# A decoder kernel on one core: the linear layer in fives and the turnings, products and low parts at other steps of a 32-step turn

## The reference, cut to what matters

```python
out = jnp.einsum('bsk,nk->bsn', data, w) + bias              # linear layer, w with blocks masked
scores = jnp.einsum('bsgrd,btgd->bgrst', xq, xk) / math.sqrt(HEAD_DIM)
probs = jax.nn.softmax(scores + mask, axis=-1)
out = jnp.einsum('bgrst,btgd->bsgrd', probs, xv)             # cross attention, 32 heads
rq = (hidden_states @ Wq.T) @ Wr.T                           # slot memory: route, take the best 8 of 256 slots
learned = gelu(h @ Wu1.T + bu1) @ Wu2.T + bu2                # its uncertainty
```

## Time and profile before

| | us |
|---|---|
| median of 3 runs | 3841.97 (3831.95 to 3848.12) |
| the profiled execution | 3841.48 |
| its span, first to last instruction | 3839.7 |
| TensorE busy | 3357.9 (87%) |
| VectorE busy | 1858.2 (48%) |
| ScalarE busy | 1296.8 (34%) |
| GpSimd busy | 826.6 (22%) |

### The profile page before, as it was taken

How to read it: one execution, slowest core, us unless ns; L and a number is a source line. 1 busy time by engine, 2 the same in 40 slices (tenths; PEclk the granted TensorE clock), 3 DMA queues, 4 the chain that set the end, 5 groups by cost and what they waited for, 6 DMA issues and landing times. The chain is left out here.

```text
span 3839.7 us, 65645 instructions
## 1 busy us (share of the span) xinstructions
PE 3357.9 (87%) x25342; PEld 2694.0 (70%) x25342; DVE 1858.2 (48%) x4790; ACT 1296.8 (34%) x3539; POOL 826.6 (22%) x700
## 2 busy tenths in 40 slices
PE   2888999987489999999947999999998299999997
PEld 2677777776278887888825878888886177777775
DVE  4577777776522222333224233332223377777775
ACT  1566666665211011111101111110111276666663
POOL 1122122211043222233202323333222000000000
PEclk9899999998599999999966999999999599999998
DMA  5756566562121111111022111111111565455541
GB/s 181 179 144 151 155 151 163 153 156 67 46 77 52 42 39 46 40 55 55 33 55 66 44 49 55 55 55 44 38 44 26 150 146 128 128 128 127 128 123 40
DMA packets 189980, 346.44 MB, mean 90 GB/s; under 512 B 27873, under 2 KB 145217, under 8 KB 189778
## 3 DMA queue, kind: packets, MB, share of 16 engines
q1 hardware_dynamic: 186032, 341.00, 33.1%
q10 hardware_dynamic: 3746, 2.79, 0.2%
HBM read 272.19 MB, written 71.51 MB: 90 GB/s over the span
## 5 line engine op out<-in xcount | busy, mean ns | idle before, releaser
L806 DVE CUSTOM_DVE_ANT_0 L_masked<-L_scores,L_nmask 112x375 f32<-112x375 f32 x1024 | 546.9, 542 | 278.2 <-PE L_scores L528 257.1
L722 ACT ACTIVATE L_probs<-L_masked,L_least 112x375 f32<-112x375 f32 x1024 | 622.6, 609 | 133.9 <-DVE L_least L806 129.7
L533 PE MATMUL L_turned<-L_ident,L_probs 112*125 112x112 f32 x3072 | 569.6, 297 | 33.2 <-DVE L_probsT L802 17.5
L1350 PE MATMUL sa_feat<-sa_x_hi,heads_w_hi 128*128 128x512 f32 (+1 forms) x1536 | 570.1, 371 | 27.4 <-POOL heads_w_lo L1323 27.4
L533 PEld LDWEIGHTS L_turned<-L_ident,L_probs 112*125 112x125 f32 x3072 | 474.0, 200 | 146.9 <-issue 53.5
L1350 PE MATMUL sa_feat<-sa_x_hi,heads_w_lo 128*128 128x512 f32 (+1 forms) x1536 | 568.0, 370 | 0.0
L1350 PE MATMUL sa_feat<-sa_x_lo,heads_w_hi 128*128 128x512 f32 (+1 forms) x1536 | 564.5, 368 | 0.0
L528 PE MATMUL L_scores<-L_krep,L_qrep 128*112 128x376 f32 x1024 | 438.6, 429 | 60.1 <-ACT L_probs L722 49.1
L717 ACT COPY L_probsT<-L_turned 125x336 f32<-125x336 f32 x672 | 291.8, 434 | 380.1 <-PE L_turned L533 377.6
L1455 DVE TENSOR_TENSOR sa_acc<-sa_acc,sa_ring 128x512 f32<-128x512 f32 x224 | 154.1, 688 | 463.2 <-PE sa_ring L1378 463.2
L1378 PE MATMUL sa_ring<-heads_p_hi,heads_o_hi 128*128 128x512 f32 x896 | 354.5, 396 | 0.0
(11 more groups left out here) (294 smaller groups left out, 5489.2 us busy)
## 6 DMA issues: line engine op xcount, KB each, us to landing
L_qrep<-query_parts SPq DMA_DIRECT2D x256, 224.0 KB, 6.4
heads_raw<-in_wqkvU_dram SPq DMA_DIRECT2D x96, 512.0 KB, 3.3
L_krep<-ctx_parts SPq DMA_DIRECT2D x256, 188.0 KB, 4.6
heads_raw<-in_wprojU_dram SPq DMA_DIRECT2D x64, 512.0 KB, 3.3
query_parts<-L_qT_hi SPq DMA_DIRECT2D x64, 224.0 KB, 3.1
query_parts<-L_qT_lo SPq DMA_DIRECT2D x64, 224.0 KB, 3.7
L_xcur<-x SPq DMA_DIRECT2D x32, 448.0 KB, 4.1
L_val<-in_ctx_dram SPq DMA_DIRECT2D x64, 187.5 KB
```

The lines of the kernel that those rows point to most:

```text
L533: mm = pe.transpose(turned[0:TC, m % 2, S * j:S * j + S], probs[0:S, m % 4, TC * j:TC * j + TC], ident[0:S, 0:S])
L722: nc.scalar.activation(probs[0:S, e % 4, :], masked[0:S, e % 3, :], ACT.Exp, bias=least[0:S, e:e + 1], scale=-1.0, accum_out=rsum[0:S, e:e ...
L806: v.tensor_tensor_reduce(out=masked[0:S, n % 3, :], in0=scores[0:S, n % 3, 0:T], in1=nmask[0:S, :], scale=1.0, scalar=HUGE, op0=ALU.add, o ...
L1350: mm = pe.matmul(feat[:, u % 2, i, 0:t.stop - t.start], a[:, u % 2, k, :], b[:, k, t], start=(n == 0), stop=(n == 3 * KT - 1))
```

## The change

In both stages work goes to other steps; no instruction's shape changes.

- Linear layer: 24 products of a half in steps 10 to 14 and 16 to 20, five a step (four in the last); VectorE's sums at 15 and 21, statistics at 16 and 21, moments at 21, next token at 24.
- First stage, queries: turnings at steps 1 and 4 (both for t+1), high parts at 2 and 5, low parts at 3 and 7; SyncE stores both halves in the turn in which they are made.
- First stage, slot memory: row turned at 15 and 20, query product at 23, its copy at ScalarE's step 25, route product at 27, hidden products six a step at 26 to 29, now into `wide[0]`; VectorE reads them at 31; slot weights turned at 5 and value product at 8, into `spare`.
- First stage, waits: TensorE waits for VectorE's weighing (`attn_read`) at 10 and 26 instead of 11 and 28.
- Second stage: query turnings at 27 and 30 (both for t+2); gated product turned at 31; output products three a step at 2 to 9, first half into `wide[0]`; result summed at 7 and 11, statistics 10 and 13, normalised at 16; row turned at 15 and 16, routing at 20 and 21, bottleneck products at 22 to 27; one row buffer.
- ScalarE's exponential stays at head n-1.

```diff
-        row = sb("row", [P, 1 if first else 2, D])
+        row = sb("row", [P, D])
...
-        Q_TURN, Q_HI, Q_LO, Q_DONE = ((28, 2), (1, 1)), ((29, 2), (2, 1)), ((30, 2), (3, 1)), (9, 1)
+        if first:
+            Q_TURN, Q_HI, Q_LO, Q_DONE = ((1, 1), (4, 1)), ((2, 1), (5, 1)), ((3, 1), (7, 1)), (9, 1)
+        else:
+            Q_TURN, Q_HI, Q_LO, Q_DONE = ((27, 2), (30, 2)), ((28, 2), (31, 2)), ((29, 2), (0, 1)), (2, 1)
...
-                if n == 11 and on(-1):
+                if n == 10 and on(-1):
                     pe.wait_ge(attn_read, w.next(attn_read))
                 if n == 24 and on(0):
                     turn_out(w, 0)
-                if n == 28 and on(0):
+                if n == 26 and on(0):
                     pe.wait_ge(attn_read, w.next(attn_read))
...
-                if n in (17, 25) and on(2):
+                if n in (16, 25) and on(2):
                     pe.wait_ge(lin_read, w.next(lin_read))
...
-                for h, n0 in ((0, 11), (1, 17)):
-                    if n0 <= n < n0 + 4 and on(2):
-                        i = 6 * (n - n0)
+                for h, n0 in ((0, 10), (1, 16)):
+                    if n0 <= n < n0 + 5 and on(2):
+                        i = 5 * (n - n0)
...
+                    if n == 23:
+                        pe.wait_ge(lo2_ok, w.next(lo2_ok))
+                        products(spare[0:BOT, 0:S], (wq_hi, wq_lo), (tT_hi, tT_lo), slice(0, S), KT, 0, 3 * KT).then_inc(query_ok, 1)
+                    if n == 27:
+                        pe.wait_ge(qaug_ok, w.next(qaug_ok))
+                        pe.matmul(spare[0:S, :], qaug[:, :], route[:, :], start=True, stop=True).then_inc(route_ok, 1)
+                    if 26 <= n < 30:
+                        i = 6 * (n - 26)
+                        mm = products(wide[0:S, 0, 0:UH], (tT_hi, tT_lo), (wu_hi, wu_lo), slice(0, UH), KT, i, i + 6)
...
+                    if 2 <= n < 6:
+                        i = 3 * (n - 2)
+                        mm = products(wide[0:S, 0, :], (z_hi, z_lo), (b_hi, b_lo), slice(0, 512), 4, i, i + 3)
+                    if 6 <= n < 10:
+                        i = 3 * (n - 6)
+                        mm = products(spare[0:S, :], (z_hi, z_lo), (b_hi, b_lo), slice(512, 1024), 4, i, i + 3)
...
-                if on(-2) and n in (10, 16):
-                    dve.drain()
-                    stats(res, 2, n // 16)
-                    if n == 16:
+                if on(-2) and n in (10, 13):
+                    dve.drain()
+                    stats(res, 2, n // 13)
+                    if n == 13:
                         moments(2)
...
-                if n in (17, 23):
-                    dve.drain()
-                    stats(xb, 0, n // 23)
-                if n == 23:
+                if n in (16, 21):
+                    dve.drain()
+                    stats(xb, 0, n // 21)
+                if n == 21:
                     moments(0)
-                if n == 26:
+                if n == 24:
                     dve.wait_ge(rstd_ok[0], w.next(rstd_ok[0]))
```

More of the change, by code:

```diff
@@ L182, in tmp @@
             return once.enter_context(nc.sbuf_tensor(f"L{layer}_once_{name}", shape, dt))
-        stage = [attn[:], row[:, 0, :], xnew[:], xcur[:]] + [buf[:].rearrange("p a t -> p (a t)") for buf in (probs, masked)]
+        stage = [attn[:], row[:], xnew[:], xcur[:]] + [buf[:].rearrange("p a t -> p (a t)") for buf in (probs, masked)]
         NST = len(stage)
@@ L431, in body @@
                     load_values(t + 1, 0)
-                if on(2):
+                if not first and on(2):
                     store_queries(w, t + 2, 0)
@@ L613, in queries, with tokens_turned, slot_ffn @@
                         turn_half(wide[:, 0, :], xnew, h).then_inc(turn_ok, 1)
-            def tokens_turned(t, half, bank):
-                turn_half(bank, row[:, (t - 1) % ROWS, :], half).then_inc(turn2_ok, 1)
-            def slot_ffn(t, w, n, on):
+            def tokens_turned(w, half, bank):
+                turn_half(bank, row, half).then_inc(turn2_ok, 1)
+            def slot_ffn(w, n, on):
                 if on(-2):
                     if n == 0:
-                        pe.wait_ge(qaug_ok, w.next(qaug_ok))
-                        pe.matmul(spare[0:S, :], qaug[:, :], route[:, :], start=True, stop=True).then_inc(route_ok, 1)
-                    if n == 11:
+                        pe.wait_ge(gate_h_read, w.next(gate_h_read))
+                    if n == 5:
                         pe.wait_ge(slot_w_ok, w.next(slot_w_ok))
@@ L627, in slot_ffn @@
                         mm.then_inc(slotT_ok, 1)
+                    if n == 8:
+                        pe.wait_ge(wT_ok, w.next(wT_ok))
+                        for j in range(2):
+                            mm = pe.matmul(spare[0:S, UH:UH + BOT], wT[:, j, :], u_val[:, j, :], start=(j == 0), stop=(j == 1))
+                        mm.then_inc(z_ok, 1)
+                    if n == 15:
+                        pe.wait_ge(z_read, w.next(z_read))
                 if on(-1):
-                    if n == 16:
+                    if n == 15:
@@ L638, in slot_ffn @@
-                    if 26 <= n < 29:
-                        i = 8 * (n - 26)
-                        mm = products(spare[0:S, 0:UH], (tT_hi, tT_lo), (wu_hi, wu_lo), slice(0, UH), KT, i, i + 8)
-                        if n == 28:
-                            mm.then_inc(gate_h_ok, 1)
-            def slot_values(w):
-                pe.wait_ge(wT_ok, w.next(wT_ok))
-                for j in range(2):
-                    mm = pe.matmul(turned[0:S, Z_HEAD % 2, TJ * S:TJ * S + BOT], wT[:, j, :], u_val[:, j, :],
-                                   start=(j == 0), stop=(j == 1))
-                mm.then_inc(z_ok, 1)
@@ L694, in body @@
                     heads_turned(w, n, on)
-                    if first and n == Z_HEAD + 4 and on(-2):
-                        slot_values(w)
                     head_scored(w, n, on)
@@ L795, in heads @@
                 m = (n - 4) % NH
-                if first and m == Z_HEAD and on(-2):
-                    dve.wait_ge(z_ok, w.next(z_ok))
-                    dve.wait_ge(z_stored, w.next(z_stored, 16))
-                    v.tensor_copy(z_row[0:S, 0:BOT], turned[0:S, m % 2, TJ * S:TJ * S + BOT])
                 if (on(0) if n >= 4 else on(-1)) and m % 3 == 0:
@@ L981, in queries @@
                             dve.sem_inc(x_free, 1)
-                if first and on(1) and n == 7:
+                if first and on(1) and n == 5:
                     dve.wait_ge(c_hi_ok, w.next(c_hi_ok))
```

174 lines of the change are left out of this document (84 added, 90 removed).

## The result

The kernel after takes 3858.23 us in the median of 6 runs (3847.72 to 3864.08), the kernel before 3842.31 beside it (3831.95 to 3848.12): a ratio of 1.0043, 95% interval 1.0024 to 1.0063. Slower, as forecast, but by 16 us where I had said 37. The profiled execution of after took 3847.72 us (span 3845.6) and lies at the lower edge of its runs. So I read turns and stretches from the traces, and whole times from the medians.

What follows compares the result with a forecast made beforehand. TensorE was taken to bound most of a turn, VectorE the first stage's light stretch. 13 x 1.75 + 13 x 1.1 = 37 us on 3841.5 gave 3878 us, own range 3862 to 3905, full range 3822 to 3932.

Steps and rivals of the forecast that it cites:

- Step 23: First stage, memory's query product moved from step 25: TensorE stalls for VectorE's late low part, +2.1 us a turn.
- Step 26: First stage, before the hidden products: TensorE stalls for VectorE's weighing, behind the next token's normalising, +1.2 us a turn.
- Step 16: First stage, wait on the linear layer's first-half sum: 0.35 of 0.69 us idle taken back a turn.
- Work changing sides: First stage: route product and a bare step join TensorE's part, other products leave; +0.1 us net a turn.
- The light stretch: First stage, steps 28 to 10: VectorE's stretch stays about 17.5 us, linear layer starts right behind the weighing; -1.3 us.
- the light stretches shrink by over 2 us: Sign that the prediction is wrong: the light stretches get over 2 us shorter.
- about 21.5: Expected sign in the first stage: score 28 to the first linear product takes about 21.5 us.
- Second stage, routing to score 27: One bare step, 0.5, and four more bottleneck products, 0.9, lengthen this TensorE part by 1.4 us a turn.
- Score 8 to routing: Second stage: row starts about 10.3 us behind score 8, quicker turnings win it back; 15.7 us against 15.77.
- The clock: Rival, both stages: one more half-clock overlap a turn, 1.9 us each, 50 us in all, 3928 us; chance 0.18.
- no change: Rival: one stall of two appears, light stretches give the rest back, +0.3 us a turn, 3850 us; chance 0.17.

Runs made afterwards that it cites:

- low_first_xnew26: The kernel after with first-stage VectorE sum, statistics and moments of the linear layer's second half behind the low part, next token at step 26: 3832.78 us, 0.9978 of before.
- linear_sixes: The kernel after with linear products six a step at 11 to 14 and 17 to 20, VectorE's first sum a step later: 3875.57 us, 1.0087 of before.
- e_row_first: The kernel after with the first stage of low_first_xnew26; second stage's last result statistics at step 15, normalising at 18, behind the row: 3806.25 us, 0.9911 of before.

## Why the prediction was right in direction and wrong in size

The kernel is slower, but by 16 us where the sum had 37, below my own range of 3862 to 3905. In turns 3 to 13 the first stage pays 0.44 us a turn where I had 1.75, and the second nothing (47.78 and 47.76) where I had 1.1. Two steps failed. In the second stage I added 1.4 us to a stretch of 14.21 us and left its half clock where it was; that half clock cost 3.17 us, and it moved: the stretch takes 12.44. In the first stage I left VectorE's light stretch at about 17.5 us; it fell by 1.10, from 18.69 to 17.59 in the mean. The other terms have errors of size only. Two figures of the prediction don't follow from its terms: 48.8 - 47.78 is 1.0 and not 1.1 us a turn, and the bounds of the terms, added up as they stand, give 3812 to 3944 us, not 3835 to 3915.

**Step 23, +2.1.** Measured +1.80, within the bounds of 1.0 and 2.6, by the mechanism named: removing VectorE's 1.7 us from ahead of the low part took 0.87 off.

**Step 26, +1.2.** Measured +0.68, mechanism right (gone with the next token back at 26). The term was oversized by the normalising: I took its 1.32 us from the earlier trace rows, and in after it lasts 0.81 in every turn. The rows of before and of after, VectorE's normalising and GpSimd's next addition:

```profile
627.16 1.29 POOL L451 TENSOR_TENSOR L_attn<-L_attn,L_xcur 112x512 f32<-112x512 f32 x1 [1.00 <-DVEq L819]
...
627.68 1.31 DVE L501 TENSOR_SCALAR L_xnew<-L_xb,L_mv,L_rstd 112x1024 f32<-112x1024 f32 x1
```

```profile
573.30 0.81 DVE L503 TENSOR_SCALAR L_xnew<-L_xb,L_mv,L_rstd 112x1024 f32<-112x1024 f32 x1
...
575.94 1.28 POOL L453 TENSOR_TENSOR L_attn<-L_attn,L_xcur 112x512 f32<-112x512 f32 x1 [5.71 <-DVEq L816]
```

Before, it runs under GpSimd's addition in 14 of its 16 turns, and the two others last 0.81; after it runs alone. In `low_first_xnew26` it is under the addition again, and lasts 1.31. The earlier trace rows had shown the same kind of instruction on the same shape at 0.81.

**Step 16, -0.35.** Measured -0.52: 0.69 idle before, 0.17 after.

**Work changing sides, +0.1.** The heavy part grew by 2.61 us, of which the three waits are 1.80 + 0.68 - 0.52 = 1.96. The remaining 0.65 is this term; I had taken it too small, though within its bound of 1.0.

**The light stretch, -1.3.** Measured -2.17. Cut at the prediction's marks, the means of the eleven turns are, before and after: score 28 to VectorE's mask of head 30, 3.67 and 3.74 us; VectorE's stretch from there to the end of the weighing, 18.69 and 17.59; from there to the first linear product, 1.25 and 0.12. So the start behind the weighing gave 1.13, close to the 1.28 I had, and by `linear_sixes` 0.6 of that is the step. What failed is "I leave VectorE's stretch at about 17.5 us". The row for 632.70 to 650.40 is one turn with half clock (0.84 granted). After, in a turn without it:

```profile
637.00:653.16 16.16, 12.60 (x138) 9.43 (x137) 15.00 (x47) 14.18 (x42) 6.76 (x7) 1.00 0.86 221
```

VectorE is busy 15.00 of 16.16 us here, so its list did not need 17.5. In after's turns with half clock the same stretch takes 16.89 to 18.75 us. The wait for the exponential before score 0 also fell by 1.08 us (1.69 to 0.61); how the 1.10 divide between this wait and the clock no run separates. The scaling of the slot weights, which I put before the weighing with 1.17 us, lasts 0.35 at its new place in every turn; before, it too ran under the addition that follows each weighing. Half clock in the first stage also fell by 54 us in all, which the sum had not in it. The sign "the light stretches shrink by over 2 us" by which I would be wrong has come. That the stretch is near the "about 21.5" of the prediction (21.44) is luck: I counted from the 22.63 us of one turn, and the mean was 23.61. Together the first stage is +0.44 us a turn where I had +1.75. Of the 1.31 us less, 0.87 are here and 0.44 in the part from the first linear product on.

**Second stage, routing to score 27, +1.4.** The work was right to a hundredth: 12.44 - 11.05 = 1.39. The step that failed is the base, and with it the clock's share, which I took as unchanged. I added 1.4 to 14.21 us of the earlier trace rows, although showed 0.51 granted in exactly that stretch. In after it runs at 1.00, and 3.17 us left it.

**Score 8 to routing, -0.1.** VectorE starts the row at 3529.65, 10.4 us behind score 8, where I had 10.3. But I then let the turnings behind it win back the whole of it. They did not: TensorE waits 2.01 us for the row, and the half clock falls in these steps. What the latter costs can be read from `e_row_first`: 14.97 us in turns without it, 16.46 with one short stretch of it, so 1.5. After at full clock would have 17.48 - 1.5 = 16.0 us here by these rows; turn 13 of `low_first_xnew26`, above, has 16.04.

So at full clock the change costs the second stage 46.15 - 44.59 = 1.6 us a turn, of which 1.39 are the products, so my 1.1 was too small there. But a half-clock stretch that cost 3.17 us was exchanged for one of about 1.5, and the turn stays where it was: 47.78 before, 47.76 after. What the stage costs comes from turns 2, 14 and 15, where before had no half clock in its products: in the traces they grow by 1.9, 3.0 and 4.3 us, while turn 0 is 4.8 us shorter up to score 27. That is 4.6 us in all; where the rest of the median's 8.1 us comes from, no profile shows. That the 8 us came as near to my 14 as they did is luck: in the turns that my sum counts there is no loss.

**The rivals.** The clock was the right thing to fear, in the wrong direction. The rival had one more overlap a turn in both stages, +50 us; half clock fell from 122 to 68 and from 86 to 64 us. By the Trainium skill, "TensorE: Matmul & The Clock Gate", section "HAM oscillation", gaps between bursts throttle the array again. The trace agrees on the place in after (behind the wait of 1.02 us and inside that of 2.01, in light steps), but one stretch moved there instead of being added. In before the clock falls with less idle time: TensorE is busy 15.02 of the 15.70 us ahead of the routing (3569.60 to 3585.30), and the earlier trace rows show 0.51 from 3587.5 on. The rival "no change" (+0.3 a turn, 3850) is nearer to the measured 3858 than my forecast: its mechanism, one stall of two, is wrong for the first stage, while "the light stretches give the rest back" is what happened.

## What to carry to other kernels

Before a moved piece of work is added to a stretch, read the granted clock of that stretch, and take out the half clock first: compare it with the same stretch in a turn that has none, often the first or the last. Then ask separately where the half clock will fall after the change, since its price depends on the place: 6.83 us of it cost 3.17 over before's products, 3.41 us cost 1.4 in the second stage's light steps of after (17.48 and 16.04), and between 0.7 and 2.6 in the first stage's (20.68 and 22.54 against 19.94), where later waits grow with it. And where TensorE waits for one result of VectorE, look at what stands ahead of it in VectorE's list: putting a sum or a statistic behind it was worth 25 to 30 us in each stage, more than the whole change.

## What the runs showed of the hardware

- A `TENSOR_SCALAR` of VectorE lasts longer under an addition of GpSimd: 1.31 against 0.81 us on 112 x 1024, 1.17 against 0.35 on 112 x 256. The Trainium skill, "VectorE: DVE Perf Modes", section "Two Vector instructions with no wait between them", calls VectorE's second read interface shared with GpSimd; the trace fits that, and gives the price to VectorE (GpSimd's addition takes 1.29 us then and 1.28 alone). That this interface is the cause no run shows.
- Seven added products a turn, whose output nobody reads, made the kernel 30 us faster (0.9926), at 0.36 us a turn of their own. In before TensorE is busy 95.45 of 100 us in this stage, and still the granted clock falls to 0.51 in it.
- The same kind of product, in steps in which TensorE also waits 1.8 us for another engine, bought nothing (1.0080; 13 us slower than after). There 1.0 us less of the wait, without added products, freed seven of twelve turns.
- The same stretch differs by 3 us between turns of one execution (16.80 and 19.70 above) by where the half clock falls. What decides it from turn to turn stays open.
